# A recurrence chunk rearranged: bias added by TensorE, squares taken from PSUM, products in a PSUM bank, one more matmul

## The reference, cut to what matters

```python
def step(carry, inp):
    W1c, b1c = carry
    xq, xk, xv, et = inp
    Z1 = xk @ W1c + b1c
    grad = _ln_l2_bwd(Z1, xv - xk, g, bb)     # mean, variance, std of Z1, then two reductions
    Attn1 = jnp.tril(xq @ xk.swapaxes(-1, -2))
    b1_bar = b1c - jnp.tril(et) @ grad
    Z1_bar = xq @ W1c - et * Attn1 @ grad + b1_bar
    W1n = W1c - (last_eta * xk).swapaxes(-1, -2) @ grad
    b1n = b1c - (last_eta * grad).sum(-2, keepdims=True)
    return ((W1n, b1n), xq + _ln(Z1_bar, g, bb, EPS_IN))
```

## Time and profile before

| what | value |
|---|---|
| median of 3 runs | 612.82 us (607.86 to 613.92) |
| the profiled execution's own time | 614.16 us |
| its span, first to last instruction | 612.3 us |
| mean granted TensorE clock | 0.754 of full speed |
| busy share of the span: PE, PEld, DVE, ACT, POOL | 80%, 57%, 77%, 57%, 54% |

### The profile page before, as it was taken

One profiled execution on the slowest core, in us unless ns is written; L12 is line 12 of the kernel. 1 busy time (PEld: TensorE's weight loads), 2 busy tenths in 40 slices (PEclk: granted clock), 3 DMA queues, 4 the chain that ended last, 5 costly groups with the idle time before them and its releaser, 6 DMA issues. The chain is left out here.

```text
span 612.3 us, 30047 instructions
## 1 busy us (share of the span) xinstructions
PE 489.4 (80%) x12294; PEld 347.4 (57%) x12294; DVE 470.1 (77%) x1574; ACT 351.6 (57%) x1164; POOL 333.5 (54%) x590
## 2 busy tenths in 40 slices
PE   0389988888467788779888898888787799959996
PEld 0144443334356677768877887777676344336663
DVE  6466888888768889998999899998997557636652
ACT  0354444323256777777777788877676477543321
POOL 1259888877444556556555655565654467430112
PEclk9999999999755755675556556665655799979998
DMA  8201111111101111111111000011010500000113
GB/s 339 97 0 36 34 35 34 36 34 40 31 23 27 27 26 35 27 27 30 31 27 26 1 1 1 18 35 35 17 35 4 162 2 1 1 1 2 70 70 138
DMA packets 15137, 24.75 MB, mean 40 GB/s; under 512 B 4228, under 2 KB 4968, under 8 KB 15080
## 3 DMA queue, kind: packets, MB, share of 16 engines
q1 hardware_dynamic: 15080, 24.10, 12.9%
HBM read 11.50 MB, written 4.19 MB: 26 GB/s over the span
## 5 line engine op out<-in xcount | busy, mean ns | idle before, releaser
L824 PE MATMUL PS<-work 32*32 32x32 f32 x4064 | 79.2, 230 | 36.0 <-DVE work L993 31.8
L824 PEld LDWEIGHTS PS<-work 32*32 32x32 f32 x4064 | 75.1, 144 | 45.7 <-issue 43.5
L1066 POOL TENSOR_TENSOR work<-work,mask 128x256 f32<-128x256 f32 x64 | 46.7, 730 | 77.4 <-DVE work L993 62.7
L813 PE MATMUL PS<-work 64*32 64x64 f32 x2048 | 67.6, 303 | 17.9 <-ACT work L1153 16.1
L813 PEld LDWEIGHTS PS<-work 64*32 64x32 f32 x2048 | 53.9, 159 | 24.8 <-issue 21.4
L836 PE MATMUL PS<-work 32*64 32x32 f32 x2016 | 64.0, 279 | 3.6 <-issue 3.6
L836 PEld LDWEIGHTS PS<-work 32*64 32x64 f32 x2016 | 55.7, 201 | 7.5 <-issue 3.7
L513 PE MATMUL PS<-X,work 128*128 128x512 f32 x128 | 58.1, 598 | 0.1
L1050 POOL TENSOR_TENSOR work<-KP,cst 128x256 f32<-128x256 f32 x64 | 39.2, 613 | 22.6 <-DVE work L951 16.9
L632 POOL TENSOR_TENSOR work<-work 128x512 f32<-128x512 f32 x32 | 43.9, 1373 | 6.7 <-DVE work L575 6.1
L1164 ACT ACTIVATE work<-TK,small 128x128 f32<-128x128 f32 x128 | 44.3, 402 | 0.0
(11 more groups left out here) (159 smaller groups left out, 1280.9 us busy)
## 6 DMA issues: line engine op xcount, KB each, us to landing
X<-in_x SPq DMA_DIRECT2D x4, 1024.0 KB, 8.0
TK<-KP SPq DMA_DIRECT2D x64, 64.0 KB, 1.9
X<-QP SPq DMA_DIRECT2D x64, 64.0 KB, 2.0
TK<-in_x SPq DMA_DIRECT2D x16, 256.0 KB, 3.0
out<-TK SPq DMA_DIRECT2D x16, 256.0 KB, 2.3
work<-in_rope SPq DMA_DIRECT2D x2, 512.0 KB, 9.2
cst<-in_consts SPq DMA_DIRECT2D x1, 289.0 KB, 5.0
work<-in_wk SPq DMA_DIRECT2D x1, 256.0 KB, 11.2
```

What stands on the lines that cost most here:

```text
L813: mm = nc.tensor.matmul(PS[HD * a:HD * a + HD, ZB[p], b * ZW:b * ZW + ZW], KT2[p][r:r + 64, k * B + b, :, :].rearrange("p e t -> p (e t)") ...
L824: mm = nc.tensor.matmul(PS[HD * a:HD * a + HD, bank, b * width:b * width + HD], AM[p][HD * a:HD * a + HD, b, part, :, :].rearrange("p e t ...
L1066: nc.gpsimd.tensor_tensor(AM[p].rearrange("p b s e t -> p (b s) e t"), S1[p].unsqueeze(2).broadcast_to([P, 2 * B, E, CS]), mask2.rearrange ...
```

## The change

- PE's `base` gets a matmul at its end that adds the copied bias `Bs` onto the Z1 columns of ZB (identity as weights, 128 moving columns). It waits for the bias copy `q["bcopy"]`. `q["base"]` is now raised by this matmul.
- DVE's L948 is gone. Everything that read Z1 now reads ZB in PSUM. The order of DVE's first steps is now: sum of squares (waits for ACT), sum, PZ, ZC.
- ACT squares straight out of ZB, waiting for `q["corr"]` in place of `q["z"]`.
- PZ, WX, ZC and the first half of `cc` move from SBUF to PSUM bank 7, which the recurrence did not use.
- PE gets `filler` behind the output part of `grads`, ahead of `base(c + 1)`: identity times 256 constant columns into unused columns of a QB bank, its result unused.

```diff
--- before.py
+++ after.py
@@ -709,7 +709,7 @@
         S1 = [carve(B * 2, CS) for _ in range(2)]
         AM = [carve(B, 2, E, CS) for _ in range(2)]
         Bs = [carve(B, HD) for _ in range(2)]
-        Z1, ZC, PZ, TS, SQ, YL, YC, WX = (carve(B, HD) for _ in range(8))
+        TS, SQ, YL, YC = (carve(B, HD) for _ in range(4))
         YY = carve(2, B, HD)
         GL = [carve(B, HD) for _ in range(2)]
         ZQ = [carve(B, HD) for _ in range(3)]
@@ -718,7 +718,7 @@
         vq = [carve(2 * B) for _ in range(2)]
         var1, sdq = [v[:, 0:B] for v in vq], [v[:, B:2 * B] for v in vq]
         lead = carve(2, B)
-        sums, cc = carve(2 * B), carve(2, B)
+        sums, cc1 = carve(2 * B), carve(B)
 
         def bc(v, n=HD):
 
@@ -726,6 +726,14 @@
 
         WB, BB, ZB, QB = 0, 2, (3, 4), (5, 6)
         ZW = HD + 2 * CS
+
+        def home(at):
+            return PS[:, 7, at * B * HD:(at + 1) * B * HD].rearrange("p (b d) -> p b d", b=B)
+
+
+        PZ, WX, ZC = (home(at) for at in range(3))
+        at = 3 * B * HD
+        cc0 = PS[:, 7, at:at + B]
 
         sq, sd = carve(J, BLK), carve(P)
         flat = lambda t: t[:, :, :].rearrange("p j n -> p (j n)")
@@ -756,7 +764,7 @@
                        4, ready=s_pre, at=ORDER, first_bank=ZB[0])
 
         with nc.Block() as block:
-            names = ("init my cy updw wcopy bcopy kt2 qt2 qr kr khx base qbase corr s1 am z p sq ss sz zc v sd r ts y yp m u u2 "
+            names = ("init my cy updw wcopy bcopy kt2 qt2 qr kr khx base qbase corr s1 am p sq ss sz zc v sd r ts y yp m u u2 "
                      "yl c w yc gl upd attn zq sqq ssq sdq rq zn zt ot").split()
             q = {n: sem(f"scan_{n}") for n in names}
 
@@ -815,7 +823,11 @@
                                     KT2[p][r:r + 64, k * B + b, :, :].rearrange("p e t -> p (e t)"),
                                     R[p][r:r + 64, k, b, :], start=(b == 0), stop=False,
                                     skip_group_check=True)
-                    mm.then_inc(q["base"], 1)
+                    pe.wait_ge(q["bcopy"], state)
+                    nc.tensor.matmul(
+                        PS[:, ZB[p], 0:B * ZW].rearrange("p (b n) -> p b n", b=B)[:, :, 0:HD], ident,
+                        Bs[1 - p if past(n, 1) else 0], start=False, stop=False, skip_group_check=True
+                        ).then_inc(q["base"], 1)
 
                 def grads(width, bank, p, part):
 
@@ -846,6 +858,11 @@
                                               start=False, stop=True, skip_group_check=True)
                     mm.then_inc(q["upd"], 1)
 
+                def filler(p):
+
+                    nc.tensor.matmul(PS[:, QB[p], 256:512], ident, ccol("spread", 0, 256), start=True, stop=True,
+                                     skip_group_check=True)
+
                 def body(c, p):
 
                     o = 1 - p
@@ -862,6 +879,9 @@
                         pe.wait_ge(q["bcopy"], done)
                         update(o)
                         grads(HD, QB[o], o, 0).then_inc(q["attn"], 1)
+                        if past(c, 2):
+                            pe.wait_ge(q["zq"], before)
+                        filler(p)
                     else:
                         base(0, 0, 1, 1)
                     if not is_last(c):
@@ -940,21 +960,13 @@
 
                 def body(c, p):
                     zb = PS[:, ZB[p], 0:B * ZW].rearrange("p (b n) -> p b n", b=B)[:, :, 0:HD]
-                    if past(c, 1):
-                        dve.wait_ge(q["corr"], c + 0)
-                    else:
-                        dve.wait_ge(q["s1"], 1)
-                    dve.wait_ge(q["bcopy"], max(c, 1) if isinstance(c, int) else c + 0)
-                    nc.vector.tensor_tensor(Z1, zb, Bs[1 - p] if past(c, 1) else Bs[0], ALU.add
-                                            ).then_inc(q["z"], 1)
-                    dve.wait_ge(q["z"], c + 1)
-                    nc.vector.tensor_tensor(PZ, Z1, g2row.unsqueeze(1).broadcast_to([P, B, HD]), ALU.mult
-                                            ).then_inc(q["p"], 1)
-                    nc.vector.tensor_reduce(sz, Z1, AX.X, ALU.add).then_inc(q["sz"], 1)
                     dve.wait_ge(q["sq"], c + 1)
                     nc.vector.tensor_reduce(ss, SQ, AX.X, ALU.add).then_inc(q["ss"], 1)
+                    nc.vector.tensor_reduce(sz, zb, AX.X, ALU.add).then_inc(q["sz"], 1)
+                    nc.vector.tensor_tensor(PZ, zb, g2row.unsqueeze(1).broadcast_to([P, B, HD]), ALU.mult
+                                            ).then_inc(q["p"], 1)
                     dve.wait_ge(q["sz"], c + 1)
-                    nc.vector.scalar_tensor_tensor(ZC, bc(sz), -1.0 / HD, Z1, ALU.mult, ALU.add
+                    nc.vector.scalar_tensor_tensor(ZC, bc(sz), -1.0 / HD, zb, ALU.mult, ALU.add
                                                    ).then_inc(q["zc"], 1)
                     dve.wait_ge(q["sd"], c + 1)
                     nc.vector.tensor_tensor(
@@ -977,17 +989,17 @@
                     nc.vector.tensor_reduce(sums[:, B:2 * B], YY[:, 1, :, :], AX.X, ALU.add).then_inc(q["m"], 1)
                     dve.wait_ge(q["u"], c + 1)
                     dve.wait_ge(q["my"], c + 1)
-                    nc.vector.scalar_tensor_tensor(cc[:, 0, :], sums[:, 0:B], -1.0 / HD, lead[:, 0, :],
+                    nc.vector.scalar_tensor_tensor(cc0, sums[:, 0:B], -1.0 / HD, lead[:, 0, :],
                                                    ALU.mult, ALU.mult).then_inc(q["cy"], 1)
                     dve.wait_ge(q["m"], c + 1)
                     dve.wait_ge(q["u2"], c + 1)
-                    nc.vector.scalar_tensor_tensor(cc[:, 1, :], sums[:, B:2 * B], -1.0 / HD, lead[:, 1, :],
+                    nc.vector.scalar_tensor_tensor(cc1, sums[:, B:2 * B], -1.0 / HD, lead[:, 1, :],
                                                    ALU.mult, ALU.mult).then_inc(q["c"], 1)
                     dve.wait_ge(q["yl"], c + 1)
                     dve.wait_ge(q["cy"], c + 1)
-                    nc.vector.tensor_tensor(YC, YL, bc(cc[:, 0, :]), ALU.add).then_inc(q["yc"], 1)
+                    nc.vector.tensor_tensor(YC, YL, bc(cc0), ALU.add).then_inc(q["yc"], 1)
                     dve.wait_ge(q["c"], c + 1)
-                    nc.vector.tensor_tensor(WX, ZC, bc(cc[:, 1, :]), ALU.mult).then_inc(q["w"], 1)
+                    nc.vector.tensor_tensor(WX, ZC, bc(cc1), ALU.mult).then_inc(q["w"], 1)
                     dve.wait_ge(q["w"], c + 1)
                     dve.wait_ge(q["yc"], c + 1)
                     nc.vector.tensor_tensor(GL[p], WX, YC, ALU.add).then_inc(q["gl"], 1)
@@ -1206,8 +1218,10 @@
                         ZT.rearrange("p b (e t) -> p e b t", e=E), ACT.Copy).then_inc(q["ot"], 1)
 
                 def body(c, p):
-                    act.wait_ge(q["z"], c + 1)
-                    nc.scalar.activation(SQ, Z1, ACT.Square).then_inc(q["sq"], 1)
+                    zb = PS[:, ZB[p], 0:B * ZW].rearrange("p (b n) -> p b n", b=B)[:, :, 0:HD]
+                    if past(c, 1):
+                        act.wait_ge(q["corr"], c + 0)
+                    nc.scalar.activation(SQ, zb, ACT.Square).then_inc(q["sq"], 1)
                     act.wait_ge(q["ss"], c + 1)
                     nc.scalar.activation(sd1, ss, ACT.Sqrt, bias=eps6, scale=1.0 / HD).then_inc(q["sd"], 1)
                     if past(c, 1):
```

## The result

The changed kernel took 628.91 us (median of 4, 627.65 to 639.38), the kernel before 612.43 us in the same comparison (median of 4, 607.86 to 613.92). The ratio is 1.0275, 95% interval 1.0205 to 1.0345: **slower by about 2.7%**. Forecast were 625 us in a range of 600 to 642, with 0.53 for slower. The profiled execution of after took 627.65 us, its span is 625.8 us. A few executions are more than 1.5% slower than the others of their kernel: medians include them, ratios leave them out, and since the profiled executions of "masked keys early" and "both, without filler" are such ones, 12 and 8 us over their medians, their chunks are used and not their spans.

What follows compares the result with a forecast made beforehand. DVE's ordered list was taken to bound the chunk. 48 chunks x (4.85 - 4.70) = +7, start +3, relapses +2 put the profiled 614.2 at 626; forecast median 625 us, range 600 to 642.

Steps and rivals of the forecast that it cites:

- The clock: TensorE in the recurrence: stays mostly at 2.4 GHz, granted clock near 1.00, since the added columns are full-array shape.
- relapses: A few short falls of TensorE's clock to the low level: +2 us in all, 0 to +10.
- The square behind the queue: ACT's square is held by earlier output steps in its queue, not by Z1; starts 1.04 us after the gradient ends.
- The hold-up of L972: DVE's targets times std (L960 before) is held by POOL's masked keys; runs from s + 0.80 to s + 1.50.
- L960 at about 0.56 us: Sign for the profile after: DVE's targets times std takes about 0.56 us, with POOL's L1050 started just ahead.
- DVE gets there first: Rival: L960 starts ahead of POOL's L1050, so POOL waits; chunk 4.55 us, kernel 608 us; chance 0.35.
- fixed piece: DVE, from the start of L971 (Y) to the end of the gradient: 2.00 us.
- The chunk: Gradient to gradient: 1.35 + 1.54 + 2.00 = 4.89 us, or 4.80 with shorter PSUM steps; taken as 4.85.
- PSUM operands dearer: Rival: seven DVE steps in line each cost 0.04 us more with PSUM operands; kernel 638 us; chance 0.06.
- PE at the low clock: PE at 0.50: the change adds 1.27 us where 0.45 is idle; chunk 5.45 us, PE the bound.
- My prices: PE matmul costs: bias add 0.42 us at 0.50 and 0.22 at 1.00; 256-column filler 0.85 and 0.44.
- The sum: Whole kernel: +7 for 48 chunks, +3 start, +2 relapses, last eight cancel; 626 us profiled, forecast 625.

Runs made afterwards that it cites:

- experiment 4: The kernel before with only the 256-column filler matmul added; 605.68 us, ratio to before 0.9885.
- experiment 5: The changed kernel without the 256-column filler matmul; 645.77 us, ratio to before 1.0495.
- experiment 2: The changed kernel with ACT's two output steps moved behind the square of Z1; 609.44 us, ratio to before 0.9946.
- experiment 1: The changed kernel with POOL's masked keys early: L1062 no longer waits for PZ; 599.61 us, ratio to before 0.9765.
- experiment 7: The changed kernel with PZ, WX, ZC and the first half of cc back in SBUF; 631.48 us, ratio to before 1.0306.
- experiment 8: The kernel of experiment 3 with PZ, WX, ZC and the first half of cc back in SBUF; 594.05 us, ratio to before 0.9695.
- experiment 9: The changed kernel with POOL's masked keys late, waiting for L972 instead of PZ; 635.28 us, ratio to before 1.0388.
- experiment 3: The changed kernel with both edits: masked keys not waiting for PZ, ACT's two output steps behind the square; 586.81 us, ratio to before 0.9578.
- experiment 6: The changed kernel with both edits (masked keys early, ACT's output steps behind the square), without the filler matmul; 600.80 us, ratio to before 0.9748.

## Why the prediction was right

The letters are the prediction's: g is the end of the gradient, s the start of the sum of squares.

**The clock.** Right. It was 1.00 in the steady part, and experiments 4 and 5 show that in these two kernels it is the filler's doing (mean 0.754 to 0.912, 0.749 to 0.945). The relapses, for which +2 us had been set aside, lie at the start: 1.00 from 178 to 191 us, 0.50 from 192 to 212 and again from 219 to 222, then 1.00 to 481.

**The square behind the queue.** Right to 0.01 us: forecast g + 1.04, measured 342.43 - 341.40 = 1.03. The sum of squares was put at g + 1.35 and stood at g + 1.32. Experiment 2 moved the queue and got the 0.40 us.

**The hold-up of L972.** Right in place, cause and size. With s = 342.72, L972 was to start at s + 0.80 and end at s + 1.50; it did so at s + 0.80 and s + 1.53. L1062 stood 0.03 us ahead of it (forecast 0.05). The line "L960 at about 0.56 us" in the list of signs didn't fit the sum, which has s + 0.80 to s + 1.50, 0.70; measured 0.73. The rival "DVE gets there first" was missed by 0.03 us, and by the same 0.02 to 0.03 in 62 of the 64 chunks. No run let L972 start first; experiment 1 shows a chunk without the hold-up, 4.45 against that rival's 4.47. The fixed piece from Y to the end of the gradient was again 346.29 - 344.29 = 2.00. One reading was wrong without a price: the prediction says that three steps moved behind the sum of squares, but ZC (L957) stood behind it in before too; only the sum and PZ moved.

**The chunk.** Worked out as 4.89, taken as 4.85, measured 4.90. The choice of 4.85 was the mis-sized term. I had taken L923's 0.25 us as a sign that reads of PSUM are shorter. That holds for L923 (now L943, again 0.25) alone; L965, L966, L969, L983 and L1005 read PSUM and take 0.28 to 0.29 each. The choice made the forecast 0.05 x 48 = 2.4 us too low.

**PSUM operands dearer.** Wrong, as its 0.06 said: experiments 7 and 8. The Trainium skill's 120 against 58 cycles ("VectorE: DVE Perf Modes", the TRN2 errata) are not to be seen in these instructions: L966, PSUM to PSUM, takes 0.29 us, and L972 out of SBUF, where nothing holds it up (experiment 1), 0.28.

**PE at the low clock.** Mis-sized. Put at 5.45 us for a fully PE-bound chunk, measured 6.11. The timeline of PE in after, in one of the few such chunks:
```profile
201.23 0.65 PE L836 MATMUL PS<-work 32*32 32x32 f32 x32 [0.72 <-POOL work L1078]
...
203.82 1.22 PE L863 MATMUL PS<-cst 128*128 128x256 f32 x2
204.97 1.08 PE L821 MATMUL PS<-work 64*32 64x64 f32 x32
205.98 0.79 PE L827 MATMUL PS<-work,cst 128*128 128x128 f32 x2
206.70 0.65 PE L900 MATMUL PS<-work 64*32 64x32 f32 x32
207.34 0.65 PE L836 MATMUL PS<-work 32*32 32x32 f32 x32
```
From start to start the filler holds PE for 1.15 us (forecast 0.85) and the bias add for 0.72 (forecast 0.42). At 1.00 the bias add takes 0.41 (344.79 to 345.20; forecast 0.22). My prices came from rows of full-size matmuls behind others of their kind; here each stands between streams of 32- and 64-row tiles and costs some 0.2 to 0.3 us more. That it is the change of shape that costs is my reading; no run separates it. Between 201.23 and 207.34 PE has no pause, and ACT waits for its bias add (timeline of ACT in after):
```profile
206.81 0.37 ACT L1199 ACTIVATE work<-PS,small 128x128 f32<-128x128 f32 x1 [2.43 <-PE PS L827]
```
Such chunks make the early part long: first seven intervals +3.2 us (forecast +3), and 48 chunks +11.1 where 48 x (4.90 - 4.70) = 9.6 accounts for most of it. Of the remaining 1.5, 1.2 lie in two of the first of the 48, which took 5.45 and 5.57.

**The sum.** Forecast +7 for 48 chunks, +3 for the start, +2 for relapses, 0 for the last eight. Measured +11.1, +3.2, nothing beside these for relapses, and +1.2, and -2 outside the recurrence, which no step had. Forecast +12 on the profiled execution, measured +13.5. That these lie so close is partly luck: the 48 chunks and the last eight cost 5 us more than forecast, and 4 of them came back where nothing was foreseen or a reserve wasn't used. Of the 4.1 in the 48 chunks, 2.4 are the choice of 4.85.

**Not foreseen.** Base (L821) now waits for the masked keys. The page's groups of after say how much (busy us and mean ns, then idle before it and its releaser):
```profile
L821 PE MATMUL PS<-work 64*32 64x64 f32 x2048 | 45.7, 230 | 22.1 <-POOL work L1062 19.6
```
These are 19.6 us over the kernel. In the usual chunk of after they are hidden, but they are paid for in experiments 5 and 9. I followed PZ to L1062 and L1062 to L972, and not on to base.

## What to carry to other kernels

When an operation is made ready earlier, look at what stands ahead of it in its engine's own queue: here two output steps nobody needed yet ate the whole gain, and moving them behind it gave 0.40 us a chunk. When work is reordered on one engine, check which instruction of a neighbour is released by each step and what it will run beside: the 0.45 us came from a neighbour's instruction that started 0.03 us ahead, and letting the neighbour start earlier was free while letting it start later was not. And a change can be a loss of 2.7% and, with two waits less, a gain of 4.2%: take its waits out one at a time before it is dropped.

## What the runs showed of the hardware

- A DVE instruction with two large SBUF inputs that starts 0.03 us behind a POOL instruction on SBUF becomes 0.73 us long in place of 0.28; by its end it looks as if it had begun 0.13 us before POOL's end (344.25 - 0.28 = 343.97, against 344.10). Started 0.37 us behind it (experiment 3), it becomes 0.40. DVE instructions with at most one large operand in SBUF kept their 0.28 to 0.29 beside it (experiment 1).
- For 128 x 128 f32, DVE takes the same 0.28 to 0.29 us in and out of PSUM and SBUF; only L943 (before L923) takes 0.25, out of PSUM. ACT's square is a little shorter out of PSUM, 0.26 to 0.28 against 0.29 to 0.31 us.
- One 256-column full-array matmul a chunk, with a result nobody reads, moves the mean granted clock from 0.754 to 0.912 (before) and from 0.749 to 0.945 (after), while PE is less busy with it than without (30.99 against 37.56 us of 40 in the same window of after and of experiment 5). Without it the mean of one variant still varied from 0.734 to 0.881 (experiment 6).
- A full-size matmul between streams of small tiles held PE for longer than behind its own kind: the 128-column pair for 0.72 us against 0.42 at 1.2 GHz and 0.41 against 0.22 at 2.4 GHz.
